# Edge passes of a graph network: weights three, sums four and accumulator five visits behind, and a one-column closing product

## The reference

```
def _gatv2(x, src, dst, edge_attr, Wl, bl, Wr, br, We, att, bo):
    xl = x @ Wl.T + bl
    xr = x @ Wr.T + br
    e = edge_attr @ We.T
    m = xl[src] + xr[dst] + e
    score = jnp.where(m > 0, m, NEG_SLOPE * m) @ att
    smax = jax.ops.segment_max(score, dst, num_segments=N)
    es = jnp.exp(score - smax[dst])
    denom = jax.ops.segment_sum(es, dst, num_segments=N)
    alpha = es / (denom[dst] + 1e-16)
    out = jax.ops.segment_sum(alpha[:, None] * xl[src], dst, num_segments=N)
    return out + bo
```

## Time and profile before

| | |
|---|---|
| median of 3 runs | 7688.16 us |
| profiled execution, its own time | 7706.77 us |
| its span | 7704.8 us |
| PE / weight loads / DVE busy | 5782.3 / 4186.0 / 4089.8 us |
| POOL / ACT busy | 3042.2 / 2572.1 us |
| mean granted TensorE clock | 0.867 |

### The profile page before, as it was taken

One profiled execution on the slowest core, in us unless ns is written; L12 is line 12 of the kernel. 1 busy time (PEld: TensorE's weight loads), 2 busy tenths in 40 slices (PEclk: granted clock), 3 DMA queues, 4 the chain that ended last, 5 costly groups with the idle time before them and its releaser, 6 DMA issues. The chain is left out here.

```text
span 7704.8 us, 170425 instructions
## 1 busy us (share of the span) xinstructions
PE 5782.3 (75%) x40520; PEld 4186.0 (54%) x40521; DVE 4089.8 (53%) x12731; ACT 2572.1 (33%) x4831; POOL 3042.2 (39%) x3157
## 2 busy tenths in 40 slices
PE   3777777777777776577777777777777698999699
PEld 2555555555555554455555555555555683222689
DVE  6455555555455555555555555555555527778532
ACT  2233333333333332333333323333333205777210
POOL 3555555555555553455555555555555000000000
PEclk9888888888888887788888888888888898999899
DMA  3333222232232332332332332332332362323479
GB/s 83 73 77 75 69 77 70 75 77 69 75 77 71 79 77 49 76 82 70 77 78 69 78 77 70 80 76 69 79 79 64 148 270 76 134 105 109 172 295 362
DMA packets 689323, 764.63 MB, mean 99 GB/s; under 512 B 368995, under 2 KB 574026, under 8 KB 664145
## 3 DMA queue, kind: packets, MB, share of 16 engines
q1 hardware_dynamic: 561781, 577.66, 24.5%
q0 software_dynamic: 100352, 102.96, 6.9%
q10 hardware_dynamic: 27102, 82.91, 2.8%
HBM read 671.04 MB, written 88.81 MB: 99 GB/s over the span
## 5 line engine op out<-in xcount | busy, mean ns | idle before, releaser
L336 POOL DMA_INDIRECT gat_rows<-rows_scr,gat_idx x3136 | 3015.6, 962 | 2862.7 <-PE gat_aps L1299 1237.0
L1290 PE MATMUL gat_tps<-ident,gat_weights 128*128 128x128 f32 x3136 | 601.2, 322 | 1319.3 <-ACTq L1155 1193.1
L1290 PEld LDWEIGHTS gat_tps<-ident,gat_weights 128*128 128x128 f32 x3136 | 384.1, 159 | 1508.1 <-ACTq L1155 1324.3
L1172 ACT ACTIVATE adj_tiles<-gat_counts 128x392 f32 (+1 forms) x784 | 390.8, 498 | 2161.2 <-remote 1135.1
L1308 PE MATMUL gat_sps<-gat_relu,gat_att 128*128 128x256 f32 x3136 | 1079.9, 478 | 0.0
L1071 DVE CUSTOM_DVE_ANT_0 gat_masked<-gat_sps,gat_miss,gat_oldtop 128x512 f32<-128x512 f32 x784 | 586.9, 749 | 754.6 <-remote 462.5
L1022 DVE TENSOR_SCALAR adj_hot_key<-adj_iota_key,adj_winbase,adj_key 128x392 bf16<-128x392 int16 x2416 | 960.5, 398 | 8.7 <-issue 8.7
L1299 PE MATMUL gat_aps<-gat_rows,gat_weightsT 128*128 128x65 f32 x6224 | 955.7, 306 | 0.0
L1299 PEld LDWEIGHTS gat_aps<-gat_rows,gat_weightsT 128*128 128x128 f32 x6224 | 938.5, 231 | 0.0
L1063 DVE COPY gat_oldtop<-gat_top 128x1 f32 x784 | 119.6, 153 | 1334.7 <-issue 622.2
L1021 DVE TENSOR_SCALAR adj_hot_lo<-adj_iota_lo,adj_low 128x128 bf16<-128x128 int16 x2416 | 636.9, 264 | 266.5 <-issue 108.4
(11 more groups left out here) (379 smaller groups left out, 6837.8 us busy)
## 6 DMA issues: line engine op xcount, KB each, us to landing
gcn_sum_adj<-adj_scr SPq DMA_DIRECT2D x98, 1568.0 KB, 8.5
gat_dstb<-dst_scr SPq DMA_DIRECT2D x784, 128.0 KB
gat_ea<-in_ea SPq DMA_DIRECT2D x784, 128.0 KB
gin_sum_adj<-adj_scr SPq DMA_DIRECT2D x49, 1568.0 KB, 8.5
adj_scr<-adj_tiles ACTq DMA_DIRECT2D x48, 1568.0 KB
at_adj<-adj_scr SPq DMA_DIRECT2D x60, 1024.0 KB, 9.5
gat_rows<-rows_scr,gat_idx POOLq DMA_INDIRECT x3136
gat_xr<-xr_scr SPq DMA_DIRECT2D x1568, 24.0 KB
```

The lines of the kernel that those rows point to most:

```text
L336: pool.indirect_dma_start(ring.rows[:, u, c, 0:ROW], None, rows_d, bass.IndirectOffsetOnAxis(ap=ring.idx[:, u, c:c + 1], axis=0)).then_inc ...
L1290: last = pe.transpose(tps[:, c * P:(c + 1) * P], wts[:, j, c * P:(c + 1) * P], ident[:])
```

## The change

The stages lag further. Transposes run three visits behind instead of two, sums four instead of three, the accumulator five instead of four. On PE the sums move from behind the transposes to the head of the visit. DVE gets a wait for `weight` of four visits before ahead of L1071, since the weights now lag. Five drain steps replace four. The product that closes the counts covers one column of the bank and one of the zero tile.

```
-    delay = {"masked": 0, "message": 0, "fifth": 0, "relu": 1, "score": 1, "top": 2, "weight": 2, "turned": 2, "evac": 2,
-             "sum": 3, "acc": 4, "topped": 3, "olded": 2}
+    delay = {"masked": 0, "message": 0, "fifth": 0, "relu": 1, "score": 1, "top": 2, "weight": 2, "turned": 3, "evac": 3,
+             "sum": 4, "acc": 5, "topped": 3, "olded": 2}

 DVE, in a visit
-                    tb, tm, ta = tiles[-4], tiles[-3], tiles[-5]
+                    tb, tm, ta = tiles[-4], tiles[-3], tiles[-6]
-                    dve.wait_ge(s["sum"], count("sum", step, 4))
+                    dve.wait_ge(s["sum"], count("sum", step, 5))
-                    dve.scalar_tensor_tensor(a, a, shrink[:, u % 4:u % 4 + 1],
+                    dve.scalar_tensor_tensor(a, a, shrink[:, (u - 5) % 4:(u - 5) % 4 + 1],
                                              aps[:, 0:D + 1], ALU.mult, ALU.add).then_inc(s["acc"], 1)
                     dve.wait_ge(s["score"], count("score", step, 2))
+                    dve.wait_ge(s["weight"], count("weight", step, 4))

 ACT, in a visit
-                j = (u - 2) % 2
-                act.wait_ge(s["turned"], count("turned", step, 2))
-                act.wait_ge(s["sum"], count("sum", step, 4))
+                j = (u - 3) % 2
+                act.wait_ge(s["turned"], count("turned", step, 3))
+                act.wait_ge(s["sum"], count("sum", step, 5))
                 act.activation(wtsT[:, j, :], tps[:], ACT.Copy).then_inc(s["evac"], 1)

 PE, in a visit (ahead of the message)
+                    j = (u - 4) % 2
+                    if not (first and u < 4):
+                        pe.wait_ge(s["evac"], count("evac", step, 4))
+                        pe.wait_ge(s["acc"], count("acc", step, 5))
+                        for c in range(GC):
+                            last = pe.matmul(aps[:, 0:D + 1], wtsT[:, j, c * P:(c + 1) * P],
+                                             rows[:, v, c, 0:D + 1].rearrange("p a f -> p (a f)"),
+                                             start=(c == 0), stop=(c == GC - 1))
+                        last.then_inc(s["sum"], 1)
 PE (behind the message; the sums that stood here are gone)
-                    j = (u - 2) % 2
-                    pe.wait_ge(s["weight"], count("weight", step, 2))
-                    pe.wait_ge(s["evac"], count("evac", step, 3))
+                    j = (u - 3) % 2
+                    pe.wait_ge(s["weight"], count("weight", step, 3))
+                    pe.wait_ge(s["evac"], count("evac", step, 4))
 PE, count_edges
-                pe.matmul(bank[:, 0:WD * NT], none[:, 0:P], none[:], start=False, stop=True).then_inc(s_window, 1)
+                pe.matmul(bank[:, 0:1], none[:, 0:P], none[:, 0:1], start=False, stop=True).then_inc(s_window, 1)
```

More of the change, by code:

```diff
@@ L35 @@
 DRAIN = 4
+CARRY = 5
 TURN = 4
@@ L1119, in _ @@
                 turn(i + TAIL // TURN, False)
-            for u in range(DRAIN):
+            for u in range(CARRY):
                 drained(u)
@@ L1291, in visits @@
                     last.then_inc(s["turned"], 1)
-                    j = (u - 3) % 2
-                    v = slice((slot + u - 3) % RING, (slot + u - 3) % RING + 1) if back is None or u >= 3 else bass.ds(back + u, 1)
-                    if not (first and u < 3):
-                        pe.wait_ge(s["evac"], count("evac", step, 3))
-                        pe.wait_ge(s["acc"], count("acc", step, 4))
-                        for c in range(GC):
-                            last = pe.matmul(aps[:, 0:D + 1], wtsT[:, j, c * P:(c + 1) * P],
-                                             rows[:, v, c, 0:D + 1].rearrange("p a f -> p (a f)"),
-                                             start=(c == 0), stop=(c == GC - 1))
-                        last.then_inc(s["sum"], 1)
                     j = (u - 1) % 2
```

74 lines of the change are left out of this document (38 added, 36 removed).

## The result

The changed kernel takes **7846.16 us** (median of four runs, 7834.06 to 7883.44), the kernel before beside it 7690.36 us (7679.8 to 7697.36): **1.0211 times before, 95% interval 1.0181 to 1.0242**. It is 156 us slower, where the likeliest case of the prediction was 131 us faster; the interval lies clear of 1, and does not say whether the loss is over 2%. The prediction's rival on the slower side came true, at six tenths of its 263 us. The profiled execution took 7883.44 us, its span is 7881.4 us.

What follows compares the result with a forecast made beforehand. PE's completions, held while POOL issues gathers, were taken to set the pace. Pairs 2364, held singles 658 and other singles 2634 gave 5656 against 5796 us; scaled, with drain, -131: 7557 us, range 7270 to 7990.

Steps and rivals of the forecast that it cites:

- likeliest case of the prediction: Whole kernel: shorter pairs of gather groups outweigh some longer visits, 131 us faster, 7557 us; chance 0.42.
- rival on the slower side: PE's transposes: their completion is caught in the hold; at two thirds of singles 263 us slower, 7951 us; chance 0.40.
- PE's completions are held while gathers are issued, and this sets the rhythm: Edge passes: others hear late of PE's finished work; 6.72 us per single gather group, 16.47 us per back-to-back pair.
- The Trainium skill's rule: SBUF ports: TensorE never waits for its ports, so gathers would not delay PE's completions; led to a rival at 6369 us.
- The 2.42 us of the weights leave PE's path: PE before the transposes: weights one visit later remove the 2.42 us from release to weights, at most 1319.3 us in all.
- Instead PE waits 0.87 us after a release: PE before the sums at the head: it waits for ACT's copy of the transposes, 0.87 us instead of 2.42.
- Sums end early after a release, so pairs come more often: POOL: sums end 1.87 us after a release, so a second gather group follows at once more often than the present 174.
- A pair gets shorter, 15.06 us: Edge passes: two gather groups back to back cost 15.06 us instead of 16.47, a cut of 1.41 us.
- A held single costs 8.43 us; 78 of them: Single gather groups after a pair: half have their transposes' completion held, so PE waits for the release; 8.43 us each, 78 visits.
- Zero product 0: PE's product closing the counts, one column instead of 392: at most 285.9 us of PE, taken as 0.
- DVE's wait for `weight` 0, drain +6: DVE's added wait delays nothing, price 0; the fifth drain step costs 3 us in each pass, 6 in all.
- The signs to look for: Profile: idle before transposes under 300 us, before sums several hundred, waited groups under 610; if slower, groups 8 to 9 us apart.

Runs made afterwards that it cites:

- gate_mid2: Changed kernel with sums between message and transposes, POOL's gather groups also waiting for the transposes, on a device that held completions: 7717.66 us, 0.9987 of the kernel before.
- gate_mid: Changed kernel with sums between message and transposes, POOL's gather groups also waiting for the transposes, on a device without the hold: 5932.89 us, 1.0010 of the kernel before.
- gate_before: Kernel before, with POOL's gather groups also waiting for the scores, on a device without the hold: 5932.54 us, 1.0002 of the kernel before.
- lag_old_place: Changed kernel with the sums put back behind the transposes, later lags and one-column product kept: 7625.03 us, 0.9883 of the kernel before.
- col: Kernel before with only the one-column zero product: 7713.26 us, 0.9999 of the kernel before.

## Why the prediction was wrong, step by step

- *PE's completions are held while gathers are issued, and this sets the rhythm.* Right where it was read, and shown by taking the gathers away: 7698 to 5791 us, the wait for weights from 1319 to 216. Too narrow: SP's steps are slower too (gate_mid2 beside gate_mid). Missed, and not to be seen in one trace: some devices, or states of them, don't show it.
- *The Trainium skill's rule.* "SBUF — State Buffer", section "SBUF: two separate sides", has TensorE never wait for a port; the prediction set it aside, since what is late is the announcement. The runs agree with that: the four transposes inside the hold at 1505.20 take 0.66 us, those of gate_before at 1505.14, without a hold, 0.65 us.
- *The 2.42 us of the weights leave PE's path.* Right: idle before the transposes 1319.3 to 3.9 us.
- *Instead PE waits 0.87 us after a release.* **This step failed first.** A release is not one instant for all: in the visit of 1504.00 the message was heard at 1508.49 and the transposes at 1510.02, 1.53 us later, and from the first to the start of the sums at 1510.74 it is 2.25 us. So the wait is as long as the 2.42 us it replaced, and the lines view has 1359.2 us before the sums where 1319.3 stood before the transposes.
- *Sums end early after a release, so pairs come more often.* **Wrong in direction**: 60 instead of 108, and 784 - 674 = 110 groups that follow at once instead of 174. The prediction contradicts itself here: it expects more than the present 174 pairs, and its sum takes 157. And its 174, read from the waits, are not all pairs: by the start times the kernel before has 108 clean ones. The sums now wait for a release of their own, after the hold, and POOL then waits for them. Pairs do come more often where the lags change and the sums stay (182, lag_old_place).
- *A pair gets shorter, 15.06 us.* Right in direction, and a little short in size: 15.73 on the mean, 15.27 in the one shown.
- *A held single costs 8.43 us; 78 of them.* The mechanism is right and the plain case costs 8.62, but all singles over 8 us have a mean of 9.06, and there are 168 where 30 had been. **With the pairs' 206 us on the other side, this term of 296 us decided the sign.** The forecast took the margin at full clock. In the visit shown, the message ended 1.27 us after the group began and the transposes 1.86 us, and both were caught; in the next one, with the clock at 0.81, the transposes ended at 1515.37, 2.75 us after its start, and were copied at 1516.12, 0.75 us later. So what gets out is not what ends within a fixed time from the start of the group, as the earlier trace rows had let me think.
- *The slower rival: above a third of the singles held, the change loses.* The mechanism came true. By its prices 168 held of 470 would have cost some 20 us; the passes grew by 153 us. A single over 8 us cost 2.36 us more than a free one and not 1.71. The count was 168 of 589 singles, well under the two thirds that its 7951 us needed; the dearer single made up for it in part. Its 0.40 and the forecast's 0.42 rested on the same margin, of which the rows showed two cases.
- *Zero product 0.* Right: the product's busy time falls from 285.9 to 132.9 us, and col gives 0.9999 (0.9974 to 1.0024).
- *DVE's wait for `weight` 0, drain +6.* Not taken apart. lag_old_place has both and is still 1.2% faster than before, so they don't outweigh the gain of the lags; their own sizes are not shown.
- *The signs to look for.* Idle before the transposes under 300 and idle before the sums of several hundred, ended by ACT's copy: both seen. Waited groups under 610: 674, the sign that the composition had gone the other way. For the slower case, groups 8 to 9 us apart were seen; a clock under 0.84 was not, it is 0.84 and 0.85 in the passes.

## What to carry to other kernels

In this kernel a wait that was removed from an engine was only worth what the next wait did not take back: ask which event ends the new wait, and whether that event is announced at the same time as the old one. Where several engines meet at semaphores in a fixed rhythm, an added wait on the pacing engine can be worth more than a removed one on the busy engine: the kernel before with POOL's groups gated behind the scores is 4.5% faster where completions are held (0.9551, 0.9505 to 0.9596) and the same where they are not (1.0002, 0.9993 to 1.0012), for one line. And a kernel is to be timed on more than one device before its order is tuned to what one trace shows.

## What the runs showed of the hardware

- On the devices where the kernel before takes 7690 to 7735 us, semaphore events of PE reach others 4.2 us late in a single group (1505.86 to 1510.02) and 6.2 us in a pair (1519.70 to 1525.87), while POOL issues indirect gathers. Without the gathers the kernel before falls from 7698 to 5791 us. In two batches the kernel before took 5931 us, with the same gathers of 963 ns, and ACT started its copies 0.04 and 0.06 us after the transposes on the mean. That is 23% of the time of a whole kernel. One batch with the hold and one without it carry the same chip number (7701.76 and 5930.6 us for before); whether that is one and the same device isn't recorded, and what makes the difference stays open.
- The granted clock goes with it: 0.84 and 0.85 in the passes with the hold, 0.96 and 0.97 without, for the same changed kernel.
- The matmul of 1 column in place of 392 is recorded with 0.17 us instead of 0.365, and takes nothing off the time (col, 0.9999).
- SP is slower as well: in one and the same kernel POOL waits 1013.6 us for SP's load of `dstb` with the hold (gate_mid2) and 41.6 us without (gate_mid), and SP takes 1.66 and 1.07 us from the issue of the indices to that of the edge attributes.
- POOL's indirect gather of 128 rows takes 963 ns of its queue and 0.30 us until the next, its plain load of 128 rows 539 ns.
